# A two-layer transformer kernel: two sets of rope tiles, and projections of q and k that wait for stores

## The reference, cut to what matters

```
x = x + attn0(layernorm(x))      # 16 q heads, 8 k/v heads, rms_norm + rope on q and k, window 1024
x = x + ffn0(layernorm(x))       # 8-bit weights, hidden 5632, silu gate
x = x + attn1(layernorm(x))      # 16 heads, segments of 512, delta-rule memory
x = x + ffn1(layernorm(x))       # hidden 8192, 2:4 sparsified activations

def apply_rope(x, positions):    # attn0 only
    x1, x2 = jnp.split(x, 2, axis=-1)
    return jnp.concatenate([x1 * cos - x2 * sin, x2 * cos + x1 * sin], axis=-1)

q = (x @ Wq).reshape(Bsz, seq, H, DK).transpose(0, 2, 1, 3)   # attn1
k = (x @ Wk).reshape(Bsz, seq, H, DK).transpose(0, 2, 1, 3)
```

## Time and profile before

| | us |
|---|---|
| runs | 39977.22 and 39404.87 |
| median of the runs | 39691.05 |
| the profiled execution | 39762.92 |
| its span on core 6 | 39761.4 |
| p0a, us from the span's start | 0 to 3270 |
| p2a, q and k | 19700 to 21250 |
| p2a, v | 21250 to 22060 |
| p3 | 29200 to the end |

### The profile page before, as it was taken

The page is one execution under the profiler, slowest core; times in us unless marked ns, Lnnn a source line. Parts: engine busy times, 40 slices in busy tenths (PEclk is TensorE's granted clock), DMA queues, the critical chain, the costliest instruction groups (busy, mean ns, idle before and its releaser), DMA issues.

```text
span 39761.4 us, 236584 instructions; the slowest of 8 cores (39141.4 to 39761.4 us)
## 1 busy us (share of the span) xinstructions
PE 19426.9 (49%) x75520; PEld 7922.0 (20%) x75520; DVE 8677.1 (22%) x19698; ACT 8943.2 (22%) x18951; POOL 1590.8 (4%) x2308
## 2 busy tenths in 40 slices
PE   5553333333246654566577222222246666666666
PEld 2221111111112221222222110000022222222222
DVE  1112222222110000000100333333332222222222
ACT  2223444444211111111200222222211111111111
POOL 0000000000000000000000000000000000000000
PEclk6665555555566666666677555555578888888888
DMA  1001000000134444444522111111134444444444
GB/s 42 27 29 34 15 15 15 15 15 15 50 110 88 89 88 81 86 89 89 114 76 70 43 38 34 33 32 32 33 100 95 84 90 84 89 84 89 84 89 76
DMA packets 2954169, 2449.69 MB, mean 62 GB/s; under 512 B 2445680, under 2 KB 2652784, under 8 KB 2794096
## 3 DMA queue, kind: packets, MB, share of 16 engines
q0 software_dynamic: 360448, 1250.05, 17.1%
q1 hardware_dynamic: 2147056, 997.56, 10.0%
q10 hardware_dynamic: 445440, 186.94, 1.7%
HBM read 1416.86 MB, written 1157.63 MB: 65 GB/s over the span
## 4 chain that ended last, share of the span: by engine, by line
PE 47%; DVE 18%; ACT 13%; ACTq 6%; issue 6%; DMA 5%; DVEq 4%; SPq 1%; another core or an unknown queue 0%; POOL 0%; POOLq 0%
PE pb L2015 7%; PE pb L1169 5%; PE pb L1923 4%; PE pb L1917 4%; ACTq L1059 4%; PE pb L1112 4%; PE pb L1118 4%; PE pb L1320 3%; ACT arena L788 2%; ACT arena L871 2%; PE pb L881 2%; DVE arena L1983 2%; PE pb L859 2%; DMA arena<-arena 2%; ACTq L1066 1%
## 5 line engine op out<-in xcount | busy, mean ns | idle before, releaser
L1112 PE MATMUL pb<-arena 128*128 128x512 bf16 x5632 | 1550.7, 439 | 3215.2 <-DMA arena<-s_xhatT 2902.7
L2015 PE MATMUL pb<-arena 128*128 128x512 bf16 x8192 | 2697.7, 502 | 428.8 <-ACT arena L2005 428.8
L1995 PE MATMUL pb<-arena 128*128 128x128 bf16 x2048 | 299.5, 300 | 3525.5 <-DVE arena L1983 3525.5
L1169 PE MATMUL pb<-arena 128*128 128x512 bf16 x5632 | 1846.7, 502 | 295.4 <-ACT arena L1159 295.4
L1917 PE MATMUL pb<-arena 128*128 128x512 bf16 x8192 | 1858.1, 380 | 60.4 <-DMA arena<-d1w 49.0
L1923 PE MATMUL pb<-arena 128*128 128x512 bf16 x8192 | 1854.7, 380 | 0.0
L1944 DVE TENSOR_TENSOR arena<-arena,pb 128x512 f32<-128x512 f32 x512 | 352.2, 688 | 6875.9 <-PE pb L1923 6875.9
L2030 ACT ACTIVATE arena<-pb 128x512 f32<-128x512 f32 x2048 | 1057.1, 603 | 2851.0 <-PE pb L2015 2851.0
L1118 PE MATMUL pb<-arena 128*128 128x512 bf16 x5632 | 1532.5, 435 | 0.0
L859 PE MATMUL pb<-arena 128*128 128x128 bf16 x5376 | 842.3, 310 | 1338.8 <-ACT arena L820 1338.8
L749 PE MATMUL pb<-arena 128*128 128x512 bf16 x1344 | 638.3, 622 | 1718.2 <-ACT arena L820 1483.2
(11 more groups left out here) (176 smaller groups left out, 26739.9 us busy)
## 6 DMA issues: line engine op xcount, KB each, us to landing
y<-arena POOLq DMA_DIRECT2D x512, 1024.0 KB, 7.9
arena<-s_xhatT SPq DMA_DIRECT2D x896, 512.0 KB, 5.9
s_xB<-arena POOLq DMA_DIRECT2D x352, 1024.0 KB, 8.4
arena<-x SPq DMA_DIRECT2D x64, 1024.0 KB, 5.1
s_xA<-arena POOLq DMA_DIRECT2D x64, 1024.0 KB, 4.1
arena<-s_xA SPq DMA_DIRECT2D x64, 1024.0 KB, 5.2
arena<-s_xB SPq DMA_DIRECT2D x64, 1024.0 KB, 5.7
arena<-g0w SPq DMA_DIRECT2D x44, 1024.0 KB, 5.2
```

The costliest lines, as they stand in the source:

```text
L1112: ins = pe.matmul(out=p.pb[bg][:], lhsT=xh_t[cur][:, dk * 128:(dk + 1) * 128], rhs=WgT[sl][:, dk * 512:(dk + 1) * 512], start=(dk == 0), s ...
L1169: ins = pe.matmul(out=p.pb[2 + dcol][:], lhsT=hT_b[cur][:, hc * 128:(hc + 1) * 128], rhs=WdT[sl][:, hc * D + dcol * 512: hc * D + (dcol + ...
L2015: ins = pe.matmul(out=p.pb[2 + dcol][:], lhsT=hT_b[cur][:, hc * 128:(hc + 1) * 128], rhs=Wd_s[sl][:, hc * D + dcol * 512: hc * D + (dcol + ...
```

## The change

In p0a there are two `qTf` and two `qTrot`, taken by turns (`gpar = g % 2`). The transposes of a group wait for the ScalarE copy of two groups before, and no longer for VectorE. The copy to `qTf[gpar]` waits for the rope sum of two groups before, and the rotation for the evacuation of two groups before. The wait of ScalarE at the end of a group is gone. VectorE gets one more drain ahead of its products. The arena grows by 2 KB.

In p2a there are two staging tiles in place of four, and the matmuls of chunk `fc` wait for the store of chunk `fc - 2` on `SP{fc % 2}` in place of the copy of chunk `fc - 1`.

In p1 and p3 the wait of GpSimd begins at a count of 48 in place of 96 and is for 32 below the count in place of 80.

```
-        self.arena = Arena(nc, 188 * 1024)
+        self.arena = Arena(nc, 190 * 1024)
-    qTf = ar.alloc([128, 512], F32)
-    qTrot = ar.alloc([128, 512], F32)
+    qTf = [ar.alloc([128, 512], F32) for _ in range(2)]
+    qTrot = [ar.alloc([128, 512], F32) for _ in range(2)]
...
                 b.wait(pe, "ac", tok_rmsevac)
-                b.wait(pe, "dv")
+                b.wait(pe, "ac", qtf_tok[gpar])
...
                 b.wait(ac, "pe", tok_tr)
-                b.inc("ac", ac.activation(out=qTf, in_=p.pb[bank_t][:],
+                b.wait(ac, "dv", rope_par[gpar])
+                b.inc("ac", ac.activation(out=qTf[gpar], in_=p.pb[bank_t][:],
                                           func=ACTF.Identity, scale=sc))
             tok_qTf = b.cnt["ac"]
+            qtf_tok[gpar] = tok_qTf
...
                 b.wait(pe, "ac", tok_qTf)
-                b.inc("pe", pe.matmul(out=p.pb[bank_r][:], lhsT=p.prot, rhs=qTf,
+                b.wait(pe, "ac", rot_tok[gpar])
+                b.inc("pe", pe.matmul(out=p.pb[bank_r][:], lhsT=p.prot, rhs=qTf[gpar],
                                       start=True, stop=True))
...
-                dv.tensor_tensor(out=r1, in0=qTf, in1=rc_s[cur], op=ALU.mult)
-                dv.tensor_tensor(out=r2, in0=qTrot, in1=rs_s[cur], op=ALU.mult)
                 dv.drain()
-                b.inc("dv", dv.tensor_tensor(out=qT_out[gpar], in0=r1, in1=r2,
-                                             op=ALU.add))
+                dv.tensor_tensor(out=r1, in0=qTf[gpar], in1=rc_s[cur], op=ALU.mult)
+                dv.tensor_tensor(out=r2, in0=qTrot[gpar], in1=rs_s[cur], op=ALU.mult)
+                dv.drain()
+                b.inc("dv", dv.tensor_tensor(out=qT_out[gpar], in0=r1,
+                                             in1=r2, op=ALU.add))
             tok_rope = b.cnt["dv"]
+            rope_par[gpar] = tok_rope
...
-            @block.scalar
-            def _(ac):
-                b.wait(ac, "dv", tok_rope)
...
-                if b.cnt.get(ch, 0) >= 96:
-                    b.wait(gp, ch, b.cnt[ch] - 80)
+                if b.cnt.get(ch, 0) >= 48:
+                    b.wait(gp, ch, b.cnt[ch] - 32)
...
-    ev = [ar.alloc([128, 512], F32) for _ in range(4)]
+    ev = [ar.alloc([128, 512], F32) for _ in range(2)]
...
-                    b.wait(pe, "ac")
+                    b.wait(pe, f"SP{fc % 2}")
...
-                    b.wait(ac, f"SP{fc % 4}")
-                    ins = ac.activation(out=ev[fc % 4], in_=p.pb[bank][:],
-                                        func=ACTF.Copy)
-                    b.inc("ac", ins)
+                    b.wait(ac, f"SP{fc % 2}")
+                    ac.activation(out=ev[bank], in_=p.pb[bank][:], func=ACTF.Copy)
                     ac.drain()
-                    b.inc(f"SP{fc % 4}", ac.dma_start(
-                        out=dstT[fc, :, tb * 512:(tb + 1) * 512], in_=ev[fc % 4]), 16)
+                    b.inc(f"SP{fc % 2}", ac.dma_start(
+                        out=dstT[fc, :, tb * 512:(tb + 1) * 512], in_=ev[bank]), 16)
```

More of the change, by code:

```diff
@@ L444, in emit_p0a @@
     cons_tok = [0, 0]
+    rope_par = [0, 0]
+    qtf_tok = [0, 0]
+    rot_tok = [0, 0]
     for i in range(NT):
@@ L574, in emit_p0a, with _ @@
             bank_t, bank_r = (0, 1) if g % 2 == 0 else (2, 3)
+            gpar = g % 2
             @block.tensor
-            def _(pe, src=src, goff=goff, bank_t=bank_t):
+            def _(pe, src=src, goff=goff, bank_t=bank_t, gpar=gpar):
                 b.wait(pe, "ac", tok_rmsevac)
-                b.wait(pe, "dv")
+                b.wait(pe, "ac", qtf_tok[gpar])
                 for j in range(4):
@@ L587, in _ @@
             @block.scalar
-            def _(ac, bank_t=bank_t, sc=sc):
+            def _(ac, bank_t=bank_t, sc=sc, gpar=gpar):
                 b.wait(ac, "pe", tok_tr)
-                b.inc("ac", ac.activation(out=qTf, in_=p.pb[bank_t][:],
+                b.wait(ac, "dv", rope_par[gpar])
+                b.inc("ac", ac.activation(out=qTf[gpar], in_=p.pb[bank_t][:],
                                           func=ACTF.Identity, scale=sc))
             tok_qTf = b.cnt["ac"]
+            qtf_tok[gpar] = tok_qTf
             @block.tensor
-            def _(pe, bank_r=bank_r):
+            def _(pe, bank_r=bank_r, gpar=gpar):
                 b.wait(pe, "ac", tok_qTf)
-                b.inc("pe", pe.matmul(out=p.pb[bank_r][:], lhsT=p.prot, rhs=qTf,
+                b.wait(pe, "ac", rot_tok[gpar])
+                b.inc("pe", pe.matmul(out=p.pb[bank_r][:], lhsT=p.prot, rhs=qTf[gpar],
                                       start=True, stop=True))
@@ L601, in _ @@
             @block.scalar
-            def _(ac, bank_r=bank_r):
+            def _(ac, bank_r=bank_r, gpar=gpar):
                 b.wait(ac, "pe", tok_rot)
-                b.inc("ac", ac.activation(out=qTrot, in_=p.pb[bank_r][:],
+                b.inc("ac", ac.activation(out=qTrot[gpar], in_=p.pb[bank_r][:],
                                           func=ACTF.Copy))
             tok_rot_e = b.cnt["ac"]
-            gpar = g % 2
+            rot_tok[gpar] = tok_rot_e
             @block.vector
```

## The result

The changed kernel takes 38,827.64 us in the median of 11 runs, the kernel before 39,773.65 us in the median of 10. The ratio is 0.977, with a 95% interval of 0.972 to 0.982. In a later set of runs, on another chip, it was 0.982 (0.972 to 0.992). The kernel is faster by about 2%, and it can't be told from these runs on which side of 2%.

The account below looks back on a forecast made before the run. Chains across engines were taken to bound the rope groups and p2a, with core 6 slowest. Saving 518 - 3 + 257 = 772 us from the 39,691 us median gave 38,920 us, range 38,620 to 39,200.

Parts of the forecast that it names:

- The rope chain: p0a rope groups: start spacing falls from 7.14 to 3.9 us, 160 times, saving 518 us.
- the first rival: p0a rope groups: clock rises in two to five groups per tile, 77 to 192 us more saved; chance 0.30.
- My sum: Whole kernel: rope 518 less 3 for drains plus 257 in p2a, 772 us saved; chance 0.44.
- q and k of layer 1: p2a projections: chunk period falls from 5.26 to 4.19 us, 240 times, saving 257 us.
- The slack that I gave the store: p2a: store of two chunks before stays hidden with 1.2 us to spare at the lower clock, 0.4 at full.
- The thresholds: Changed GpSimd waits in p1 and p3: change nothing, priced at 0.
- a gain over 2%: Whole kernel: time below 38,897 us; chance 0.49, against 0.50 within 2% and 0.01 slower.
- The landing store: Rope and p2a: late-landing stores replace the removed waits, time about 39,300 us, or 39,100 with one; chance 0.12.
- the lower upper clock spreads: p0a and p2a: core 6's dense work at 1.00 drops to 0.81, costing about 80 us; chance 0.12.
- the rule that the prediction weighed: Whole die: held at 13/16 of the clock, 0.81, while three or more of its cores run dense matmuls.

Follow-up runs that it names:

- the run that exposed it: Only p2a changed on the kernel before: two staging tiles, matmuls waiting for the store of the chunk just before; 40,290 us, 1.8% above the kernel before.

## Why the prediction was right

**The rope chain** came out as worked out: the transposes go in behind the rotation, the start spacing is 3.83 to 3.88 us at a clock of 0.50, against 3.9 predicted, and VectorE's sums trail by a group. What was mis-sized is the term: 518 us predicted, 606 to 616 measured from first to last rotation. About 10 us of the difference are the period, 3.84 and not 3.9; the other 80 to 90 are the first rival, to which I had given 0.30. In 29 to 52% of the rotations, by core and profile, the clock has risen, and the spacing there is 2.82 us at 0.81 or 2.52 at 1.00, where I had written 2.7. My sum and that rival were not two cases but both true, in different groups of the same tile. The right forecast was the sum plus the lower bound of the rival, 77 us.

**q and k of layer 1** came out as predicted: 1.07 us for each of 240 chunks was 257 us; the stretch is 223 to 289 us shorter by the comparison taken. The slack that I gave the store, 0.4 or 1.2 us by the clock, is what the traces have, 0.45 and 1.2; the waits for it sum up to 0.3 and 5.1 us on the cores read.

**The thresholds** are worth nothing that shows, 0.998 (0.995 to 1.001).

**The time.** 38,920 us were predicted against a median of 39,691 for the kernel before. Measured were 38,828 and 39,774, 946 us apart in place of 772. That the time itself is off by 92 us only is in part luck, since the kernel before came out 83 us above the median that I started from. Of the 174 us about 95 are the rope groups, most of it their risen clock; the rest is no more than the medians scatter. I had given 0.49 to a gain over 2% and 0.50 to one within; the ratio, 0.977 and 0.982 in the two sets, leaves that open.

**The rivals.** The landing store did not take the place of the removed waits; the run that exposed it shows what it would have cost: 646 us, of which 492 are the holes and 158 the clock that falls across them. That the lower upper clock spreads with the change is not shown. The first profile of the changed kernel spoke for it: p3 took 11,070 to 11,376 us on all cores, against 10,491 to 10,599. But all that changed in its code is the threshold that is worth nothing, the second profile has 10,484 to 11,023, and kernels that don't touch p0a have up to 11,015 and 11,114. In q and k, 38% of the matmuls ran at full clock in the kernel before, 46 and 52% in the changed one. What makes the clock of a core 0.81 or 1.00 in p3 was not settled; it is worth up to 890 us, as much as the change.

## What to carry to other kernels

A wait for everything issued on an engine costs the whole chain between the engines; name the one event that frees the buffer, and price the step by the start spacing of what stays in the loop. Before moving an instruction ahead in an in-order queue, ask what stands behind it while it waits. Where TensorE's idle time is shortened, work out the period at both clocks, because fewer holes may raise it; and if a gap of several microseconds must stay, matmuls without a use in it can pay for the stage behind it. A new hole of some microseconds has to be priced together with the clock that may fall behind it.

## What the runs showed of the hardware that was not expected

The clock rises across holes. In the rope groups of the changed kernel TensorE is busy 9.16 of 12.00 us with holes of 0.93 to 0.98 us, and the granted clock goes from 0.50, the level of 1.2 GHz, to 1.00, that of 2.4 GHz, at the fourth group in this tile, anywhere from the second to the sixth in others, and in a few not at all (2 of 32 tiles on core 6 of the second profile, 7 on core 0). No row of the kernel before had shown this. The Trainium skill (TensorE: Matmul & The Clock Gate, "What's actually happening") says that activity releases the throttle; here the trace agrees, and the activity had holes of a quarter of a period, while attention 0 with 53% stayed low in the stretch of the earlier trace rows.

A pair of float32 matmuls of 512 columns takes 2.04 us at 0.50, 1.31 at 0.81 and 1.10 at 1.00; four float32 transposes take 1.06, 0.70 and 0.60 us.

Holes of 2.94 us between chunks let the clock fall often: 35% of the matmuls ran at the lower level (5.03 us for 16 of them in place of 3.61). Holes of 0.9 to 1.5 us in the run with extra matmuls seldom did: 1 to 7% of the rotation pairs of a core take 2.0 us.

The middle level of 0.81 comes and goes by pairs of cores, and not by the half of four. The second profile of the changed kernel shows it in p3, cores 4 and 6 (length, busy us of PE, PEld, DVE, ACT, POOL, granted clock, DMA share, GB/s):

```profile
35500.00:38000.00 2500.00, 1609.81 (x5602) 645.19 (x5709) 583.71 (x1760) 427.07 (x769) 150.58 (x218) 0.69 0.41 77
35500.00:38000.00 2500.00, 1555.89 (x6344) 656.75 (x6344) 648.45 (x1956) 474.82 (x855) 160.92 (x230) 0.83 0.45 85
```

Core 5 has 0.69 as core 4 has, core 7 has 0.83 as core 6 has, and cores 0 to 3 have 0.82 or 0.83. The shares of time at 0.81 in p3 agree within 0.01 for the cores of a pair in all profiles and differ by up to 0.40 between the two pairs of a die (cores 0 to 3, or 4 to 7). So the rule that the prediction weighed, of a whole die, has the size of the step right, but these runs show it for two cores at a time. What sets it off they do not show.
